# Column additions and row work moved from VectorE to GpSimd in a four-layer graph network kernel

## The reference

```python
edge_index = jnp.stack([src, dst])
...
Q = jax.nn.relu(x @ query_kernel + query_bias)[row]
K = jax.nn.relu(x @ key_kernel + key_bias)[col]
V = (x @ kernel)[col]
...
att = jnp.sum(Qh * Kh, axis=-1)
alpha = segment_softmax(att, row, num_nodes)      # exp(att - largest att of the row), divided by its sum
msg = Vh * alpha[:, :, None]
out = jax.ops.segment_sum(msg, row, num_segments=num_nodes)
out = out.reshape(num_nodes, UNITS)
out = out + bias
...
x = _layernorm(x + out, axis=-1)                   # the second layer, as the reference applies it
```

## Time and profile before

| | us |
|---|---|
| median of three runs | 2523.57 (2522.58 to 2524.35) |
| the profiled execution | 2524.51 |
| its span | 2522.7 |
| counting, 30 to 458 | 428 |
| attend, 1415 to 2178 | 763 |

### The profile page before, as it was taken

How to read it: one execution, slowest core, us unless ns; L and a number is a source line. 1 busy time by engine, 2 the same in 40 slices (tenths; PEclk the granted TensorE clock), 3 DMA queues, 4 the chain that set the end, 5 groups by cost and what they waited for, 6 DMA issues and landing times. The chain is left out here.

```text
span 2522.7 us, 38976 instructions
## 1 busy us (share of the span) xinstructions
PE 2167.6 (86%) x12483; PEld 921.4 (37%) x12570; DVE 1981.2 (79%) x2690; ACT 1186.5 (47%) x1579; POOL 89.3 (4%) x147
## 2 busy tenths in 40 slices
PE   5888988899688888888888689898988889699998
PEld 3555555466332222222222222222222222255555
DVE  7887878333399999999999699898999989743223
ACT  4676766466511112111210587787877879300000
POOL 1000000110000000000000000000000000211000
PEclk9998999999799999999999899999999999899999
DMA  0000000266700000000000444344444434200000
GB/s 20 0 0 0 0 0 0 76 207 228 227 21 6 6 6 9 6 6 6 9 6 3 108 122 108 105 122 112 119 113 114 115 103 125 56 1 1 1 9 18
DMA packets 266004, 144.83 MB, mean 57 GB/s; under 512 B 169469, under 2 KB 260883, under 8 KB 265900
## 3 DMA queue, kind: packets, MB, share of 16 engines
q1 hardware_dynamic: 265094, 143.04, 20.3%
q10 hardware_dynamic: 806, 0.40, 0.1%
HBM read 103.43 MB, written 39.97 MB: 57 GB/s over the span
## 5 line engine op out<-in xcount | busy, mean ns | idle before, releaser
L1297 DVE CUSTOM_DVE_ANT_0 ps<-ps,max_mask 128x1536 f32<-128x1536 f32 (+1 forms) x400 | 700.7, 1864 | 14.5 <-PE ps L1251 14.5
L1550 DVE SCALAR_TENSOR_TENSOR counts<-counts,att_a 128x1792 f32<-128x1792 f32 x263 | 518.3, 2029 | 38.9 <-ACT counts L1530 38.9
L1530 ACT ACTIVATE counts<-ps 128x896 f32<-128x896 f32 x526 | 454.2, 916 | 180.9 <-PE ps L1474 179.4
L1474 PE MATMUL ps<-att_q,att_k 99*128 99x448 bf16 x1400 | 339.5, 366 | 49.6 <-issue 24.2
L1284 ACT ACTIVATE max_mask<-counts 128x3136 uint8 x24 | 67.6, 2816 | 528.6 <-DVE max_mall L1305 528.6
L480 ACT ACTIVATE counts<-ps 128x899 f32 x261 | 247.2, 947 | 135.5 <-PE ps L430 121.9
L1483 PE MATMUL ps<-counts,att_v 128*32 128x448 f32 x2104 | 260.6, 568 | 36.5 <-DVE counts L1550 8.1
L1474 PEld LDWEIGHTS ps<-att_q,att_k 99*128 99x128 bf16 x1400 | 110.4, 99 | 382.3 <-issue 169.9
L1251 PE MATMUL ps<-counts,max_q 96*128 96x512 bf16 (+1 forms) x700 | 170.0, 360 | 74.2 <-DVE max_mx L1297 52.2
L426 PE MATMUL ps<-hot 128*128 128x192 bf16 (+1 forms) x474 | 201.7, 442 | 32.3 <-DVE hot L331 32.3
L615 PE MATMUL ps<-counts 128*128 128x512 bf16 (+1 forms) x1036 | 205.7, 358 | 20.6 <-DVE counts L683 19.9
(11 more groups left out here) (209 smaller groups left out, 2471.6 us busy)
## 6 DMA issues: line engine op xcount, KB each, us to landing
att_k<-keys SPq DMA_DIRECT2D x175, 198.0 KB
att_v<-values SPq DMA_DIRECT2D x175, 128.0 KB
counts_turned<-counts SPq DMA_DIRECT2D x25, 784.0 KB, 5.0
att_a<-counts_turned SPq DMA_DIRECT2D x175, 112.0 KB
max_q<-queries SPq DMA_DIRECT2D x25, 192.0 KB, 3.0
att_q<-queries SPq DMA_DIRECT2D x7, 519.8 KB
queries<-fl_cuts SPq DMA_DIRECT2D x24, 128.0 KB
keys<-fl_cuts SPq DMA_DIRECT2D x24, 128.0 KB
```

Source lines behind the costliest of these rows:

```text
L1297: v.tensor_tensor_reduce(out=flat[:, lo:hi], in0=flat[:, lo:hi], in1=mask[slot][:, lo:hi], scale=1.0, scalar=0.0, op0=ALU.mult, op1=ALU.ma ...
L1474: last = nc.tensor.matmul(m.bank[2 * (n % NS) + z][:, 0:CW], k[i][:, 2 * h + z, :], q[:, 2 * h + z, :], start=True, stop=True)
L1530: nc.scalar.activation(e[n % NE][:, :, :], m.ps[:, 2 * (n % NS):2 * (n % NS) + 2, 0:CW], ACT.Exp).then_inc(exped, 1)
L1550: v.scalar_tensor_tensor(w, w, 1.0, a[i % DG][:, :].unsqueeze(1).to_broadcast([P, 4, CW]), op0=ALU.min, op1=ALU.mult).then_inc(weighed, 1)
```

## The change

In counting, POOL gets a program of its own that does the 261 column additions; DVE loads no positions any more and does nothing but rounds; ACT loads its positions four at a time instead of sixteen. Between maxima and attend, the separate block is gone: attend's own program makes the negated rows, and for chunk 0 three DMAs from ACT's queue place them in the queries straight from SBUF; SP issues the first queries, without those rows, at once, then slot 0, bias and input rows. In attend the queries come in four DMAs, one for each pair of heads, each behind its own score wait. POOL adds input and bias, adds the sum, subtracts the mean and multiplies by the root; DVE keeps the reciprocals, the weighted rows and the statistics.

```diff
-            def add(g, s, base):
-                v.wait_ge(bank_free, g + 1 + 4)
-                v.wait_ge(added, g + NSH)
-                column = m.counts[:, :, ds(base, 1)]
-                v.tensor_tensor(column, column, shared[s], op=ALU.add).then_inc(added, 1)
...
+        @block.gpsimd
+        def _(pool):
+            bad = pool.value_load(t.bad[0:1, 0:1], min_val=0, max_val=1)
+            with pool.If(bad == 0):
...
+                    for k in range(n):
+                        pool.wait_ge(bank_free, BG * i + k + 1 + 4)
+                        pool.wait_ge(added, BG * i + k + NSH)
+                        column = m.counts[:, :, ds(base[k], 1)]
+                        pool.tensor_tensor(column, column, shared[k % NSH], op=ALU.add).then_inc(added, 1)
...
+                        if k % LOADED == 0:
+                            base = nc.values_load_multi_w_load_instructions(
...
-            load_queries(0, 0)
-            load_queries(0, 1)
+            for h in range(HP):
+                load_queries(0, h)
+            load_slot(0, 0, 0)
             sp.dma_start(bb[:, :], bias.unsqueeze(0).to_broadcast([RB, D])).then_inc(b_loaded, 16)
             load_rows(0)
...
-                hold(sp, scored, PB * (c + 1) - (HP - 1), m.passed)
-                load_queries(c + 1, 0)
-                hold(sp, scored, PB * (c + 1), m.passed)
-                load_queries(c + 1, 1)
+                for h in range(HP):
+                    hold(sp, scored, PB * (c + 1) - (HP - 1) + h, m.passed)
+                    load_queries(c + 1, h)
...
+            for c in range(NC):
+                pool.wait_ge(x_loaded, 16 * (c + 1))
+                pool.tensor_tensor(xr[:, :, :], xr[:, :, :], bb[:, :].unsqueeze(1).to_broadcast([RB, RPC, D]),
+                                   op=ALU.add).then_inc(pool_step, 1)
+                pool.wait_ge(pool_step, 2 * c + 1)
+                pool.wait_ge(weighted, 2 * c + 2)
+                pool.tensor_tensor(y[:, :, :], y[:, :, :], xr[:, :, :], op=ALU.add).then_inc(mixed, 1)
                 inverse_roots(pool, m, mv, sd, normed, rooted, c)
+                pool.tensor_tensor(y[:, :, :], y[:, :, :], wide(mv[:, :, 0]), op=ALU.subtract).then_inc(pool_step, 1)
+                pool.wait_ge(rooted, 2 * c + 2)
+                pool.wait_ge(pool_step, 2 * c + 2)
+                pool.tensor_tensor(y[:, :, :], y[:, :, :], wide(sd[:, :]), op=ALU.mult).then_inc(finished, 1)
...
+            act.wait_ge(neg_copied, 1)
+            for z in range(3):
+                act.dma_start(q[KS + z:KS + z + 1, :, :], neg[z * HEADS:(z + 1) * HEADS, 0:CW]).then_inc(neg_placed, 16)
...
                 weights(c + 1, 1, range(1))
-                rows(c)
+                weigh_rows(c)
                 weights(c + 1, 1, range(1, 2))
+                weights(c + 1, 2, range(1))
+                statistics(c)
+                weights(c + 1, 2, range(1, 2))
```

More of the change, by code:

```diff
@@ L49 @@
 NSH = 8
+LOADED = 4
 HOT = T * (WG * (SB + TB) + 2 * P)
@@ L358, in _, with rounds @@
                 one_hots(NH - 1, NH - 1).then_inc(col_ready, 1)
[L360 to L363, removed]
+                def rounds(i):
                     for q in range(BB):
                         make(BB * i + q + NH, q % NH)
[L366 to L375, removed]
+                with v.Fori(0, NBODY) as i:
+                    rounds(i)
                 for r in range(BB * NBODY + NH, NU):
                     make(r, r % NH)
-                for g in range(left, NTG):
-                    add(g, g % NSH, base[g - left])
             with v.Else():
@@ L1392, in attend @@
         names = ("b_loaded x_loaded scored exped weighed summed acc_ready turned step "
-                 "normed rooted finished stored out_free turned_used").split()
+                 "normed rooted finished stored out_free turned_used pool_step weighted mixed").split()
         sems = {n: ctx.enter_context(nc.semaphore("att_" + n)) for n in names}
         (b_loaded, x_loaded, scored, exped, weighed, summed, acc_ready, turned, step,
-         normed, rooted, finished, stored, out_free, turned_used) = (sems[n] for n in names)
-        q_loaded = [ctx.enter_context(nc.semaphore(f"att_q{i}")) for i in range(2)]
+         normed, rooted, finished, stored, out_free, turned_used, pool_step, weighted, mixed) = (sems[n] for n in names)
+        neg_names = "neg_step neg_clipped neg_turned neg_copied neg_placed neg_stored".split()
+        neg_step, neg_clipped, neg_turned, neg_copied, neg_placed, neg_stored = \
+            (ctx.enter_context(nc.semaphore("att_" + n)) for n in neg_names)
+        pcs = acc_y[:, 0:SB * 3 * HEADS // 2].bitcast(BF16).rearrange("p (b k h) -> p b k h", k=3, h=HEADS)
+        neg = more[:, :, :].rearrange("p z n -> p (z n)").bitcast(BF16)[0:3 * HEADS, 0:ND]
+        q_loaded = [ctx.enter_context(nc.semaphore(f"att_q{i}")) for i in range(HEADS // 2)]
         slot_loaded = [ctx.enter_context(nc.semaphore(f"att_slot{i}")) for i in range(DG)]
@@ L1516, in chunk @@
                             sums(c, d, d < 2, d >= 2 * SB - 2)
+            pe.wait_ge(neg_step, 5)
+            for b in range(SB):
+                last = nc.tensor.matmul(m.bank[b // 4][0:3 * HEADS, (b % 4) * P:(b % 4 + 1) * P],
+                                        pcs[:, b, :, :], m.identb[:, :], start=True, stop=True)
+                if b in (3, SB - 1):
+                    last.then_inc(neg_turned, 1)
+            pe.wait_ge(neg_copied, 3)
+            pe.wait_ge(neg_placed, 48)
             for c in range(NC):
@@ L1525, in _ @@
         def _(act):
+            act.wait_ge(neg_copied, 1)
+            for z in range(3):
+                act.dma_start(q[KS + z:KS + z + 1, :, :], neg[z * HEADS:(z + 1) * HEADS, 0:CW]).then_inc(neg_placed, 16)
+            act.wait_ge(neg_turned, 2)
+            nc.scalar.activation(neg[:, 4 * P:16 * P].rearrange("p (k n) -> p k n", n=4 * P), m.ps[0:3 * HEADS, 1:4, :],
+                                 ACT.Copy).then_inc(neg_copied, 1)
             for n in range(NC * PB):
+                if n == NE - 2:
+                    act.wait_ge(neg_stored, 48)
+                    act.wait_ge(neg_placed, 48)
                 if n >= NE:
@@ L1553, in rest @@
             def rest(c):
-                for i in range(2, SB):
+                for i in range(3, SB):
                     weights(c, i)
@@ L1561, in take_sums, with weigh_rows @@
                 v.tensor_copy(acc[:, :, :], m.ps[:, 2 * NS:2 * NS + 2, 0:CW]).then_inc(acc_ready, 1)
-            def rows(c):
-                s = Steps(v, step, (6 + RPC + 1) * c)
+            s = Steps(v, step)
+            half = D // 2
+            def weigh_rows(c):
                 v.wait_ge(turned, c + 1)
```

149 lines of the change are left out of this document (61 added, 88 removed).

## The result

The changed kernel takes 2528.55 us (median of 14 runs) and the kernel before 2524.27: a ratio of 1.002, 95% interval 1.0013 to 1.0028. It is slower by some 4 us, at the edge of what counts as a change. The profiled execution has a span of 2526.4 for 2522.7, so 3.7 more. Behind this small sum stand a gain of 48 us and a loss of 52.

A forecast was written before the change was run, and what follows sets the result against it. PE, with holes from DVE's loads, was taken to bound counting, DVE attend. −35.3 − 12.1 + 52.8 + 1.1 + 0.7 = +7.2 on the profiled execution's 2524.5 gave, set against the runs' median, 2531 us; range 2478 to 2545.

The forecast's parts named there:

- Counting: Counting stage: with the load of positions off DVE, PE's 15 holes close; −35.3 us, bounds −30 to −36.
- The rival that GpSimd's additions are the bound: Counting: POOL's additions set the pace from 1.64 us each; at 2.0 the kernel takes 2660 us; chance 0.04.
- Start: Start of attend: SP issues the first queries at the end of maxima, first scores 12.1 us earlier; bounds −14 to −10.
- The race: Start of attend: negated rows, copied by about 1398 and placed by three DMAs, must be there by first scores at 1400.3.
- late negated rows: Start of attend: negated rows late there was named as a sign that the prediction is wrong.
- The chain: Attend's chunk boundaries: POOL finishes 9.7 us after the statistics, SP's tile 5 load and (5,0) come late; +8.8 each, +52.8 for six.
- The first rival: Attend's boundaries: POOL is not held by the halves, finish 3.6 us after the statistics, 2.7 a boundary; 2494 us; chance 0.25.
- The second: Attend's boundaries: the wait for tile 5 costs nothing and DVE stays the bound, −2.5 a boundary; 2463 us; chance 0.11.
- The last: Attend's boundaries: POOL gets only every second gap between halves, 7.7 us more a boundary; 2577 us; chance 0.05.
- the first small step: Attend's boundaries: POOL's first of four steps after the statistics passes at once; the other three each wait one half of 2.03 us.
- Queries by pairs: Attend's boundaries: first scores go when the first quarter of queries has landed; 0.9 us gained each, between 0 and 1.44.
- Input plus bias in chunk 0: Attend, chunk 0: POOL's addition falls among DVE's halves and holds them for up to 1.1 us; +1.1.

The follow-up runs named there:

- count_alone: Kernel before with the counting change alone (additions on GpSimd, positions on ScalarE four at a time): 2488.63 us, ratio 0.9858.
- dve_waits: Changed kernel with one wait more: after the statistics VectorE holds half (2,1) back until GpSimd has finished the rows: 2493.91 us, ratio 0.9879.
- sp_later: Changed kernel with SP issuing the loads of tiles 5 to 9 ahead of the store of finished rows and next input rows: 2469.95 us, ratio 0.9781.
- rows_dve_sp: Changed kernel with all row work back on VectorE and SP's store and row load behind the loads of tiles 5 to 9: 2468.80 us, ratio 0.978.
- add_one: Kernel before with the counting change alone, plus one 128x128 product on GpSimd ahead of every column addition: 2489.98 us, ratio 0.9866.
- queries_two: rows_dve (changed kernel, all row work on VectorE) with queries in two DMAs, as before, chunk 0's included: 2477.87 us, ratio 0.9817.
- rows_hidden: rows_dve (changed kernel, all row work on VectorE) with half (1,1) put between statistics and normalised rows: 2468.49 us, ratio 0.9777.
- two_back_sp: Changed kernel with SP's order of sp_later and only the last two row steps (mean and root) back on VectorE, behind half (2,1): 2468.54 us, ratio 0.9778.
- phase: two_back_sp with the input rows loaded ahead of the wait for the store's landing: one run of 2469.22 us.

## Why the prediction was right, point by point

**Counting.** The load of positions was the cause of the 15 holes; −35.3 was forecast, and count_alone gave −36.3. That the load made them, and not the additions, is seen in the trace of before, where PE's 15 holes end with VectorE's one-hots:

```profile
PE ps L426 <- DVE hot L331: 32.3, 15, 2.2
```

Each falls at a load: one load lasts from 87.12 to 90.74, VectorE's next round starts at 91.00, and PE, idle since 90.46, goes on at 92.69. ScalarE's loads of four take 0.31 us (66 of them, by the trace of after), not 0.9. The forecast had taken VectorE's 3.6 us for ScalarE's loads of sixteen too, but these took 1.02 in the trace of before, so much less had to be hidden than it thought. The rival that GpSimd's additions are the bound fell at this size, but by less than its chance of 0.04 suggests: one product of 128x128 more, and GpSimd was busy 1.41 of 1.47 us.

**Start.** −12.1 was forecast, −11.7 came. The race was near, as the forecast said, but the sum followed the wrong runner: it went by SP's loads, and in the trace the negated rows were last. PE's first scores, at 1364.53, are released by their placement in the queries, after 4.45 us of idle time. That the size is right to 0.4 us is in part luck; late negated rows were one of the signs of being wrong that the forecast named.

**Boundaries.** The chain held link by link: 9.5 us for 9.7 to the finish, 11.3 for 10.9 on to (5,0), 3.19 for 3.25 to the next half. dve_waits shows that halves hold the steps, sp_later that SP's place behind the finish turns this into time, rows_dve_sp that this order is free otherwise. The first rival (GpSimd is not held) falls with dve_waits. The second (tile 5's wait costs nothing) is what sp_later makes true by another order, at 2470 where 2463 was worked out. The last (only every second gap) is not seen; the finish would have come some 7.7 us later than it did.

Over six boundaries, by the starts of the halves in the two traces, the terms are these. A chunk's first half follows the half before it 1.1 us sooner (0.9 forecast); (5,0) then comes 6.9 later than before all the same (7.5); the half behind it adds 1.2 (1.3); and the next one adds 0.4 on average, 0.8 at three of the six, which the forecast did not have. That makes 8.4 for 8.8.

**What was off inside it.** The forecast let the first small step pass and gave three halves to the other three. In the trace all four are longer than they are without halves in dve_waits, by 1.69, 1.65, 0.94 and 1.60, which makes 5.9 for the 6.1 forecast. The size came out; the way it is spread did not. And only two of the four lengthen a half: the last of the three within 6.74 us and the one behind it take 2.86 each, for 2.02. GpSimd's sum (L1427) had also lengthened half (1,1) to 2.85, which the forecast left out; it fell mostly into the 1.3 us for which VectorE would have stood there, 0.17 of which is left. The rule of the Trainium skill (page "SBUF — State Buffer", section "Who interferes with whom") that a VectorE instruction with two inputs in SBUF contends with a GpSimd instruction that reads SBUF agrees with dve_waits (3.3 us for four steps that take 9.2 beside halves). The same section of the Trainium skill also calls the shared ports an exclusive lock. By the estimate above, add_one has some 150 us of such instructions side by side, so here whatever is locked is not locked for their whole measured length.

**Mis-sized terms.** Queries by pairs were taken at 0.9 a boundary and measured 1.1 in the changed kernel's own trace and 1.2 to 1.6 by queries_two; the finish comes that much sooner with it, as the forecast had it. Input plus bias in chunk 0 was priced at 1.1 and cost nothing: it runs from 1364.30 to 1365.56, ahead of the first half at 1367.31. The forecast's bounds are added wrongly at the upper end: its terms at their upper bounds give 2547, not 2544. Nothing in the result hangs on it.

No version run here is clearly better than rows_dve, the counting, the start and the queries of the change with the row work left on VectorE: 2468.49 us, 2.25% under the kernel before. rows_dve_sp, rows_hidden, two_back_sp and sp_later are within 1.5 us of it.

## What to carry to other kernels

Before small work goes from a full engine to an idle one, ask whether the two can run side by side at all: here steps of 3.3 us took 9.2, and running them beside the full engine's work was what made them slow. Then follow the signal that the moved work raises: six microseconds of lateness cost little by themselves, until a queue that works in strict order stood on that signal ahead of a load that PE, ScalarE and VectorE all needed. A sum near zero can hide two large terms, and undoing the one that costs was worth 60 us.

## What the runs showed of the hardware that was not expected

In two_back_sp one GpSimd addition of 112x512, 1.26 us alone, lasted 67 to 69 us in six of seven chunks, and in phase 69 to 71 us in five, with 2.3 us in a sixth. It ended about when VectorE's row of halves first broke off (in the first case at 1574.82, where VectorE idled from 1573.69). In sp_later the same addition beside halves took 1.5 to 2.4 us, and in the changed kernel GpSimd got in at halves' ends. So that GpSimd gets a turn between instructions that follow each other without a gap is no fixed rule here. Another moment of arrival, in phase, did not change it in five of six chunks, and what decides stays open. It cost no time, since the sum was not needed until the chunk's end.

After 13 us without work PE's products took 1.68 us for four where 0.93 is usual, at a granted clock of 0.50 (1.2 GHz) until 1506. PE's scores at the first boundary of after:

```profile
1503.20 1.68 PE L1441 MATMUL ps<-att_q,att_k 99*128 99x448 bf16 x4
...
1506.25 0.93 PE L1441 MATMUL ps<-att_q,att_k 99*128 99x448 bf16 x4
...
1508.01 0.93 PE L1441 MATMUL ps<-att_q,att_k 99*128 99x448 bf16 x4
```

From 1499.94 on they begin 3.26, 3.05 and 1.76 us apart, with PE busy for 5.26 of the 5.30 us at the low clock. So a half's work on PE takes some 3.2 us there, more than the 1.94 that VectorE needs, and 1.76 at 1.00, less than it. A stall here costs more than its own length: the halves behind it came 3.19 and 2.75 us apart.
